# Attention steps taken in pairs on TensorE, rows of maxima written by three engines, negation at step 7

## The reference, cut to what matters

```python
# x: (1, 2048, 128), 16 heads of 64
q, k, v = heads(x @ Wq), heads(x @ Wk), heads(x @ Wv)
w = softmax(q @ k.T / sqrt(64))
out = merge(w @ v) @ Wo + bo
x = layernorm(x + out)
```

## Time and profile before

| | us |
|---|---|
| runs | 1854.48, 5277.4, 2946.83 (median 2946.83) |
| profiled execution, own time | 1861.61 |
| its span, first to last instruction | 1860.4 |
| first scores of the attention start at | 440.8 |
| last sums of the attention start at | 1702.7 |
| mean granted TensorE clock | 0.909 of full; 1.00 in all stretches of 80 us from 560 to 1600 us |

### The profile page before, as it was taken

One profiled execution on the slowest core, in us unless ns is written; L12 is line 12 of the kernel. 1 busy time (PEld: TensorE's weight loads), 2 busy tenths in 40 slices (PEclk: granted clock), 3 DMA queues, 4 the chain that ended last, 5 costly groups with the idle time before them and its releaser, 6 DMA issues.

```text
span 1860.4 us, 33373 instructions
## 1 busy us (share of the span) xinstructions
PE 1636.5 (88%) x12745; PEld 844.1 (45%) x12745; DVE 1168.0 (63%) x1948; ACT 1324.3 (71%) x1745; POOL 1306.7 (70%) x670
## 2 busy tenths in 40 slices
PE   4888862667999999999999999999999999996795
PEld 3666642654344444444444444444444444432475
DVE  2566667456576666766667666677666766633476
ACT  2455530353798898888989888889889888885223
POOL 2233331421899999999999998999999999995422
PEclk7588855777999999999999999999999999998698
DMA  8000000210000000000000000000000000001312
GB/s 244 3 3 4 3 1 8 62 43 1 12 12 12 24 12 12 12 12 24 12 12 12 12 24 12 13 12 12 18 18 12 12 12 20 16 12 30 99 39 73
DMA packets 69942, 46.08 MB, mean 25 GB/s; under 512 B 36412, under 2 KB 61488, under 8 KB 69784
## 3 DMA queue, kind: packets, MB, share of 16 engines
q1 hardware_dynamic: 61368, 35.77, 7.1%
q0 software_dynamic: 2496, 5.13, 0.9%
q10 hardware_dynamic: 5920, 3.04, 0.8%
HBM read 34.58 MB, written 9.34 MB: 24 GB/s over the span
## 4 chain that ended last, share of the span: by engine, by line
PE 72%; DVE 10%; DMA 5%; issue 5%; POOL 4%; ACT 3%; ACTq 1%; another core or an unknown queue 0%; DVEq 0%; POOLq 0%; SPq 0%
PE psum L1915 24%; PE psum L1902 22%; PE psum L1873 6%; DMA max_rows<-a_nm 3%; PE psum L1525 2%; PE psum L1923 1%; PE psum L1846 1%; DVE a_mx L2091 1%; DMA a_Mb<-max_rows 1%; POOL a_acc L2198 1%; POOL y_rows L1090 1%; PE psum L465 1%; PE psum L470 1%; PE psum L1535 1%; PE psum L375 1%
## 5 line engine op out<-in xcount | busy, mean ns | idle before, releaser
L2198 POOL TENSOR_TENSOR a_acc<-a_acc,a_Pb 128x1024 f32<-128x1024 f32 x448 | 1066.5, 2381 | 98.4 <-ACT a_Pb L2013 43.3
L2091 DVE TENSOR_REDUCE a_mx<-psum 128x2 f32<-128x1024 f32 x512 | 625.9, 1225 | 323.8 <-PE psum L1873 320.2
L2027 ACT ACTIVATE psum<-a_Mb 128x1024 f32<-128x1024 f32 x510 | 524.8, 1029 | 89.9 <-DMA a_Mb<-max_rows 44.2
L2013 ACT ACTIVATE a_Pb<-psum 128x1024 f32<-128x1024 f32 x512 | 520.8, 1017 | 59.9 <-PE psum L1902 57.7
L1915 PE MATMUL psum<-a_Pb,a_Vb 128*64 128x512 f32 x2048 | 553.7, 619 | 10.2 <-issue 9.7
L1902 PE MATMUL psum<-a_Qh,a_Kh 64*128 64x512 f32 x1024 | 257.3, 498 | 6.7 <-ACT psum L2027 5.2
L1902 PEld LDWEIGHTS psum<-a_Qh,a_Kh 64*128 64x128 f32 x1024 | 96.1, 184 | 367.3 <-issue 283.2
L1873 PE MATMUL psum<-a_Kh,a_Qh 64*128 64x512 f32 x1024 | 206.8, 399 | 13.2 <-DVE a_mx L2091 13.0
L1902 PE MATMUL psum<-a_Ql,a_Kh 64*128 64x512 f32 x1024 | 204.2, 394 | 0.0
L1902 PE MATMUL psum<-a_Qh,a_Kl 64*128 64x512 f32 x1024 | 203.0, 392 | 0.0
L1915 PEld LDWEIGHTS psum<-a_Pb,a_Vb 128*64 128x64 f32 x2048 | 102.2, 135 | 198.4 <-issue 185.3
(11 more groups left out here) (388 smaller groups left out, 1911.2 us busy)
## 6 DMA issues: line engine op xcount, KB each, us to landing
a_Mb<-max_rows SPq DMA_DIRECT2D x31, 512.0 KB, 4.5
x_rows<-att_raw ACTq DMA_DIRECT2D x2, 1483.5 KB, 25.4
g_w<-in_L_ffn_w_eDF_dram SPq DMA_DIRECT2D x2, 1408.0 KB, 8.4
r_W<-in_L_ffn_W_dram SPq DMA_DIRECT2D x1, 2048.0 KB, 15.3
r_tile_x<-x_rows SPq DMA_DIRECT2D x23, 64.5 KB
g_tile_x<-x_rows SPq DMA_DIRECT2D x23, 64.5 KB
y_all<-y_rows SPq DMA_DIRECT2D x4, 256.0 KB, 3.9
g_w<-in_L_ffn_w_eFD_dram SPq DMA_DIRECT2D x2, 512.0 KB, 9.4
```

The costliest lines, as they stand in the source:

```text
L2013: act.activation(b.Pb[:, step % BUFS, :], ps[:, slot:slot + 2, :].rearrange("p a b -> p (a b)"), ACT.Exp, scale=SCALE).then_inc(S["probs"], 1)
L2027: act.activation(ps[:, slot:slot + 2, :].rearrange("p a b -> p (a b)"), b.Mb[:, U % 2, :], ACT.Copy).then_inc(S["seeded"], 1)
L2091: v.tensor_reduce(b.mx[:, :, qc, quarter:quarter + 1], ps[:, bank:bank + 2, :], AX.X, ALU.max).then_inc(S[f"free{bank}"], 1)
L2198: g.tensor_tensor(b.acc[:, u, :], before, b.Pb[:, step % BUFS, :], ALU.add).then_inc(S["added"], 1)
```

## The change

TensorE goes through the steps in twos: both scores, the even step's maximum jobs, the products with V of the two steps before, the odd step's maximum jobs, then the odd job of either. Which engine writes a step's row depends on the step: VectorE for steps 2, 4 and 14 of a unit, TensorE for 9, 10 and 12 (a pair of matmuls with the constant 1/64 as weights and `Mb` as moving operand, in place of a waiting), ScalarE for the other ten. `Mb` is held as fp32r. The maxima run 7 instead of 9 steps ahead, so the negation stands at step 7, and the first unit has its 16 early jobs in 7 steps. The odd jobs move by one or so: keys to step 0, queries to 2, sums to 5, output to 12; reciprocals to 5, 5, 7, 8; normalise to 9, VectorE's output to 13. The load of `Mb` waits for the scores rather than the rows of the unit before last. `inverted`, a semaphore, is replaced by VectorE's own chain.

```diff
-INVERT = (4, 5, 6, 7)
-AHEAD = 9
+INVERT = (5, 5, 7, 8)
+SEED_DVE, SEED_PE = (2, 4, 14), (9, 10, 12)
+AHEAD = 7
...
 def misc_job(step):
-    if i == 1 and p < PAIRS - 1:
+    if i == 0 and p < PAIRS - 1:
         return "k", p + 1, qt
-    if i == 3 and U < UNITS - 2:
+    if i == 2 and U < UNITS - 2:
         return "q", U + 2
-    if i == 4 and U:
+    if i == 5 and U:
         return "sum", U - 1
-    if i == 11 and U:
+    if i == 12 and U:
         return "out", U - 1
...
 def max_jobs(step):
-    first = NT - AHEAD
     if U == 0 and i < AHEAD:
-        jobs = [(1, 2 * i), (1, 2 * i + 1)] if i < first else [(1, first + i)]
+        jobs = [(1, m) for m in range(NT * i // AHEAD, NT * (i + 1) // AHEAD)]
     else:
-        jobs = [(U + 2, i - AHEAD) if i >= AHEAD else (U + 1, first + i)]
+        jobs = [(U + 2, i - AHEAD) if i >= AHEAD else (U + 1, NT - AHEAD + i)]
...
+def seeder(step):
+    if step < 2:
+        return "begin"
+    return "dve" if step % NT in SEED_DVE else "pe" if step % NT in SEED_PE else "act"
...
 attention_rows_sp:
         if U > 1:
-            sp.wait_ge(S["seeded"], seeds_of(NT * (U - 1) - 1))
+            sp.wait_ge(S["scores"], NT * (U - 1))
...
 attention_pe, scores(step):
-        if step > 1:
-            pe.wait_ge(S["seeded"], seeds_of(step))
+        who = seeder(step)
+        if who == "pe":
+            rows_ready(U)
+            pe.wait_ge(S["probs"], step - 1)
+            for h in range(2):
+                pe.matmul(ps[:, slot + h, :], b.mean[HEAD[h], :], b.Mb[HEAD[h], U % 2, h * QT:(h + 1) * QT], start=True, stop=False, skip_group_check=True)
+        elif who != "begin":
+            pe.wait_ge(S[f"seeded_{who}"], seeds_of(step))
...
-    for step in range(STEPS):
+    for step in range(0, STEPS, 2):
         scores(step)
+        scores(step + 1)
         for _, U, m in max_jobs(step):
             maximum(U, m)
-        if step > 1:
+        if step:
             weigh(step - 2)
-        if misc_job(step):
-            misc(misc_job(step))
+            weigh(step - 1)
+        for _, U, m in max_jobs(step + 1):
+            maximum(U, m)
+        for job in (misc_job(step), misc_job(step + 1)):
+            if job:
+                misc(job)
...
 attention_act:
     def seed(step):
+        if seeder(step) != "act":
+            return
...
-        key = misc_job(step)
+        key = misc_job(step - 1) if step else None
         if key and key[0] in "qkv":
             {"q": queries, "k": keys, "v": values}[key[0]](*key[1:])
-        if i == 8 and U:
+        if i == 10 and U:
             normalised(U - 1)
...
 attention_dve:
+    def seed(step):
+        U, slot = step // NT, 2 * (step % 2)
+        if seeder(step) != "dve":
+            return
...
+        v.wait_ge(S["probs"], step - 1)
+        v.tensor_copy(ps[:, slot:slot + 2, :].rearrange("p a b -> p (a b)"), b.Mb[:, U % 2, :].bitcast(F32)).then_inc(S["seeded_dve"], 1)
...
         for _, unit, m in max_jobs(step):
             maximum(unit, m)
-        if i == 2 and misc_job(step - 1):
+        if step + 2 < STEPS:
+            seed(step + 2)
+        if i == 1 and misc_job(step - 1):
             keys(*misc_job(step - 1)[1:])
-        if i == 3 and misc_job(step):
+        if i == 3 and U < UNITS - 2:
             queries(U + 2)
...
-        if U and i == 8:
+        if U and i == 9:
             normalise(U - 1)
         if U and i == 10:
             normalised_low(U - 1)
-        if U and i == 11:
+        if U and i == 13:
             output(U - 1)
```

More of the change, by code:

```diff
@@ L1751, in adds_of @@
     return 15 * (step // NT) + max(step % NT, 1)
+def seeder(step):
+    if step < 2:
+        return "begin"
+    return "dve" if step % NT in SEED_DVE else "pe" if step % NT in SEED_PE else "act"
 def seeds_of(step):
-    return step - 1
+    return sum(seeder(s) == seeder(step) for s in range(step + 1))
 def allocate_attention_weights(k):
@@ L1804, in attention_rows_sp @@
         if U > 1:
-            sp.wait_ge(S["seeded"], seeds_of(NT * (U - 1) - 1))
-        sp.dma_start(b.Mb[:, U % 2, :], bcast(rows.rearrange("h c p -> (h c p)").unsqueeze(0), [P, 2 * QT])).then_inc(S["rows_in"], 16)
+            sp.wait_ge(S["scores"], NT * (U - 1))
+        sp.dma_start(b.Mb[:, U % 2, :].bitcast(F32), bcast(rows.rearrange("h c p -> (h c p)").unsqueeze(0), [P, 2 * QT])).then_inc(S["rows_in"], 16)
 def attention_weight_act(k, m):
@@ L1887, in seed, with rows_ready @@
         end(last, 0)
+    def rows_ready(U):
+        if U:
+            pe.wait_ge(S["rows_in"], 16 * U)
+        else:
+            freed(("seed", 0))
     def scores(step):
@@ L2036, in attention_act @@
     act.activation(b.ident[:, :], k.ident[:, :], ACT.Copy)
+    act.activation(b.mean[:, :], k.ones[:, :], ACT.Copy, scale=1.0 / D)
     residual_norm_act(k, 1)
@@ L2102, in negate @@
         v.tensor_reduce(b.nm[:, :, :], b.mx[:, :, :, :], AX.X, ALU.max, negate=True).then_inc(S["negated"], 1)
+    def seed(step):
+        U, slot = step // NT, 2 * (step % 2)
+        if seeder(step) != "dve":
+            return
+        if U:
+            v.wait_ge(S["rows_in"], 16 * U)
+        else:
+            bank, n = plan.at["seed", 0]
+            v.wait_ge(S[f"free{bank}"], n)
+        v.wait_ge(S["probs"], step - 1)
+        v.tensor_copy(ps[:, slot:slot + 2, :].rearrange("p a b -> p (a b)"), b.Mb[:, U % 2, :].bitcast(F32)).then_inc(S["seeded_dve"], 1)
     def invert(U, part):
@@ L2106, in invert @@
         at = slice(part * P, (part + 1) * P)
-        v.reciprocal(ps[:, bank, at], ps[:, bank, at]).then_inc(S["inverted"], 1)
+        dve.did(v.reciprocal(ps[:, bank, at], ps[:, bank, at]))
     def normalise(U):
-        v.wait_ge(S["inverted"], 4 * U + 4)
+        dve.wait()
         v.wait_ge(S["heads_out"], U + 1)
@@ L2152, in attention_dve @@
             maximum(unit, m)
-        if i == 2 and misc_job(step - 1):
+        if step + 2 < STEPS:
+            seed(step + 2)
+        if i == 1 and misc_job(step - 1):
             keys(*misc_job(step - 1)[1:])
-        if i == 3 and misc_job(step):
+        if i == 3 and U < UNITS - 2:
             queries(U + 2)
         if U and i in INVERT:
-            invert(U - 1, INVERT.index(i))
-        if U and i == 8:
+            for part in range(4):
+                if INVERT[part] == i:
+                    invert(U - 1, part)
+        if U and i == 9:
             normalise(U - 1)
```

5 lines of the change are left out of this document (3 added, 2 removed).

## The result

| | before | after |
|---|---|---|
| runs | 1854.48, 5277.4, 2946.83, 1855.66 | 1838.87, 1835.35, 1830.31, 1837.13 (median 1836.24) |
| profiled execution, own time | 1861.61 | 1838.87 |
| its span | 1860.4 | 1837.3 |
| first scores of the attention start at | 440.82 | 441.51 |
| from there to the second unit's first add | 59.30 | 66.48 |

The two long runs of before are disturbed and are left out. The ratio is 0.9894, interval 0.9852 to 0.9936: the change makes the kernel 1.1% faster, which is inside the 2% that the forecast called "within 2%". The profiled execution went down by 22.8 us where 29 were forecast. By the table 27.6 us were won in the 30 regular units and 3.3 at the end; 7.2 were lost in the first unit and 0.7 by a later start.

What follows compares the result with a forecast made beforehand. TensorE was taken as the bound, with GpSimd close behind; afterwards GpSimd at 37.86 us per unit instead of 38.83 saves 29 us over 30 units, first unit 0: 1861.6 - 29 = about 1832 us, range 1816 to 1866.

Steps and rivals of the forecast that it cites:

- within 2%: Whole kernel: the forecast gain of 29 us lies under the 37 us a measurement can tell; chance 0.76.
- Form borders: TensorE's rounds: changing matmul form costs 0.35 us, now once per two steps; saves 2.8 us per unit, jobs return 1.0.
- GpSimd takes over at 37.86 per unit: Regular units: GpSimd's adds become the bound, 37.86 us per unit instead of 38.83, 29 us over 30 units.
- the 0.1 on top of the floor: Regular units: GpSimd's floor of 37.76 us, raised to 37.86 because two servers this close lose a little.
- TensorE 37.2: Regular units: TensorE's own work after the change, 37.2 us per unit, bounds 36.8 and 38.3; 37.5 with small waits.
- ScalarE's rows: Six of 16 rows per unit leave ScalarE: no gain alone, but ScalarE needs about 30 us instead of 36.
- Negation at step 7: Row of maxima arrives earlier: ScalarE's 1.4 us wait per unit goes, and TensorE's pause, up to 0.5 per unit.
- VectorE's copies: Rows at steps 2, 4 and 14: a copy from SBUF to PSUM takes 1.15 us, range 0.7 to 1.4.
- Rival C: Regular units: VectorE's copies block GpSimd's adds, 41.2 us per unit, +71 us, 1933 us in all; chance 0.05.
- First unit: First unit of attention: extra exposed maxima cost 3.8 us, rounds give back 2.8; bounds -5 and +4, taken as 0.
- The end stays: End of the stage: unchanged, the last sums still wait 6.10 us for GpSimd's last add.

Runs made afterwards that it cites:

- half_adds_new: The kernel after, with GpSimd's adds, except the first of each unit, over half the width: 1815.5 us, 0.9699 of before, unit 37.82 us.

## Why the prediction was right, and where it was wrong

The forecast time was 1832 us and the profiled execution took 1839; the median is 1836, inside the range, and "within 2%" was the likeliest outcome. The step that failed is the first unit, which the sum took at 0: it took 7.2 us more. By the runs, 4.5 of these are three more of VectorE's reductions for which TensorE stands, and the rest goes with a lower granted clock. In the regular units the mechanism held in the main, with TensorE tied to GpSimd where the sum had it 0.26 us faster.

- *Form borders.* Forecast: a round 3.93, a job 1.11, the sums 1.21, TensorE rows 0.23 each. Measured: 3.92, the first pair behind a job 0.11, 5.13 for the round with the sums, a row 0.22; a round with a projection 5.01, so 1.09 for the job. Right to 0.02.
- *GpSimd takes over at 37.86 per unit.* Measured 37.91; 27.6 us of the 29 forecast came. The size is right, in part by luck: the 0.1 on top of the floor was meant for two servers that lose a little, but GpSimd runs without a gap, and its adds come 2.53 us apart in the middle of the stage, against 2.52 in the unit from which the floor was read. And "TensorE 37.2" was a mean over all units. By the same prices a unit with all four jobs and the sums is 8 x 3.93 + 0.7 + 4 x 1.11 + 1.21 = 37.8, and 23 of the 32 units are such (1 to 23). The mean hid that TensorE ties with GpSimd there, which is why half_adds_new won nothing in the middle. The same slip stands in the view of before: with five jobs its unit is 16 x 2.14 + 5 x 0.90 = 38.74 by the same prices (38.6 in the shortest units), and units 1 to 23 take 38.96 on average. The rest for ScalarE's wait is 0.2 to 0.4 there, and the lengths follow the wait, as shown above.
- *ScalarE's rows "earn nothing alone, keep ScalarE from taking TensorE's place".* Right for TensorE's three, and larger than it sounds: without them the unit is 38.8. Wrong for VectorE's three, which the kernel can do without; ScalarE at 13 rows is fast enough when the three at 9, 10 and 12 are TensorE's.
- *Negation at step 7: "up to 0.5 per unit".* Right for the old order, too small for the new: with it back at 9 the unit is 2.5 us longer, 1.7 where the granted clock stays at 1.00. I priced the wait at the 1.4 us of the old order; in the new one it is 2.6. An edit's price was read in the schedule that the change does away with.
- *VectorE's copies.* 1.15 forecast, 1.217 measured. Rival C, that they hold up the adds, is out: 96 copies, and the 448 adds keep their duration:

```profile
L2243 POOL TENSOR_TENSOR a_acc<-a_acc,a_Pb 128x1024 f32<-128x1024 f32 x448 | 1066.4, 2380 | 89.4 <-ACT a_Pb L2039 26.0
```

  The Trainium skill's condition for the mode by which the prediction had a copy lock GpSimd out ("VectorE: DVE Perf Modes", Mode 2×_2P: source and destination in SBUF) is not met by a copy into PSUM, and the trace agrees, with 2380 ns an add here against 2381.
- *First unit: "bounds -5 and +4; I take 0".* The failed step. It took 7.2 us more, outside its own bounds. The term set two more exposed reductions (3.8 us) against 2.8 us of saved borders and a reduction hidden in each round. In the trace TensorE stands for ten reductions instead of seven, 14.5 us instead of 10.0; at the same granted clock the new order takes 4.3 to 5.0 us more than the old (66.1 to 66.8 beside 61.8), so hardly anything of the saved borders is left. The clock had no term: it was 0.82 in this execution and 0.86 in that of before, and the same program at 0.89 took 62.7, so over half of the 7.2 comes and goes with the execution. How much of the saved borders was given back by the added rows and jobs, and how much lay beside the reductions, was not separated.
- *The end stays.* 3.3 us less from the last unit's first add on. TensorE's last wait for GpSimd grew from 6.10 to 13.37 us, as TensorE was done sooner.

Adding up: -1.6% was forecast, -1.1% measured (-1.5 to -0.6). The profiled execution missed the forecast by 6.3 us: +7.2 in the first unit, +1.4 in the units, +0.7 in a later start, -3.3 at the end, and 0.3 outside the span and in rounding.
